# Self attention values: two heads of a pair in one set of PSUM rows, and the norm split over ScalarE, VectorE and GpSimd

## The chip, the cores and the metric

The kernel runs on one core of one Trainium2 chip. The metric is device time in microseconds (us), the median of several executions of the whole program; less is better. Engines: PE is TensorE (matrix products and transposes, results in PSUM), PEld its weight loads, DVE is VectorE, ACT is ScalarE, POOL is GpSimd, SP issues DMAs. Each engine runs its own instructions strictly in the order written and waits at semaphores.

## What is computed

A decoder of four layers on x of 16 batches x 256 rows x 128 columns, in float32; each layer is a self attention, a cross attention and an expert layer. Five attentions over x itself (the first layer's and, beside its cross attention, a second one; the second and the third layer's; and one in the third layer's expert part) have 16 heads of 8 columns. Without their projections, masks, gates and rotary turns they are one function; the third layer applies it three times, each time with the last result as queries:

```
scores = jnp.einsum('bthd,bshd->bhts', q, k * scale) + mask
attn = jax.nn.softmax(scores, axis=-1)
return jnp.einsum('bhts,bshd->bthd', attn, v)
...
context = _self_attention(q, k, v, mask)
for _ in range(REPETITIONS - 1):
    context = _self_attention(context, k, v, mask)
```

## The kernel before, in words

`program` builds stages s0 to s12 and lets each engine run its part of one after the other. Five of the stages are a `SelfAttention`: s0 (rope, no mask), s1 (causal, and 64 rows of cross attention beside it), s3 (a position bias and a gate), s6 (mask added, three repetitions) and s8 (causal, rope). A stage works in units: one batch, all 16 heads; s6 has 48 units (16 batches x 3 repetitions, in groups of four batches, so a unit's next repetition is four units later), the others 16. Two batches are a chunk of 512 rows, for which projections are made. A new unit starts every 8 slots (10 in s1). `pe_slot`, `act_slot`, `dve_slot`, `pool_slot` and `sp_slot` write out what an engine does in slot g: each line there asks whether some unit is now at a given offset. So the offsets fix the order of each queue.

Offsets of a unit: slots 0 to 7, row maxima of the scores, two heads in each slot (`pe_max`, `dve_max`; the score banks handed back by the maxima); slot 9 (`MBT`), the negated maxima are turned (PE L694), copied to `MT` by ACT (L703), and SP copies them beside the queries in `SKB` (`sp_self_shift`, L1245). Slots 12 to 19 (`LE` = 12): scores again with the maxima in them (PE L1452), exponentials (ACT L1412); `pe_pv` (L1505) at 15, 17, 19 and 21 multiplies with the values `VA`, which hold 8 columns and a column of ones a head, so the ninth column is the sum of the softmax.

The results of pv gather in PSUM bank 6 (`PS[:, 6]`), four heads each in rows 32 i to 32 i + 8 of two half banks. When half of the unit's heads are there, ACT copies the bank to `TV` (L718), PE turns it into bank 7 with four transposes (`pe_tvt`, L727), and VectorE makes the reciprocals of the sums (L738) and two products (L744) from bank 7 into `OO`. This happens twice a unit, turns at slot 18 and slot 22. Bank 7 serves all such turns and projections, one after the other: who takes it (`pj_take`) waits for the reader before. In slot `OOS` = 23 (24 with the gate, 26 with cross) PE turns `OO` (L767), ACT copies it to `OT` (L777). Slot OOS + 1 (`OUT`) starts the tail of a chunk: output projection, residual, norm.

Queries and keys are split into three bf16 parts by ACT (`act_hi`, `act_mid`: L638, L644) and GpSimd (`pool_rest`, `pool_lo`: L649, L655), in `HH`, and SP copies them into `SKB` by `stack` (L668), twelve copies a split. In s6 the output `OT` of a unit that has another repetition is split this way in slot OOS and the next; SP's four first copies are step 0 in slot OOS + 1 = 24 (slot 0 of the unit three later), the other eight step 1 in slot 25 (its slot 1). In `sp_slot` the line of the maxima (`MBT`) stands ahead of the steps of a split. The scores of the next repetition wait for the copies to land (`stacked`).

Of the kernel before, what the change touches and what calls it, by code (L numbers as in the profile page):

```python
# [73 lines left out]
class Chip:  # L74


    def __init__(self, nc, A, ctx):
# [19 lines left out]
        self.VA = [sb(f"VA{i}", [128, 64, 9]) for i in range(3)]  # L97
# [3 lines left out]
        self.M3 = [sb(f"M3{i}", [128, 16, 4]) for i in range(2)]  # L101
        self.MB = [sb(f"MB{i}", [128, 2, 32], BF16) for i in range(2)]
# [5 lines left out]
        self.OC = sb("OC", [128, 2, 128])  # L108
# [87 lines left out]
class Begin:  # L196
# [312 lines left out]
class Heads:  # L509
# [222 lines left out]
    def dve_normalise(self, e, f, oo, half):  # L732

        K = self.K
        v = K.PS[:, 7, :].rearrange("p (q x k) -> p q x k", q=2, x=8)
        r = K.RC[f % 2][:, 0:16].rearrange("p (q x o) -> p q x o", q=2, o=1)
        e.wait_ge(*self.tvt.at(f))
        e.reciprocal(r, v[:, :, :, 8:9]).then_inc(*K.dv.inc())  # L738
        e.wait_ge(*K.dv.now())
        v = K.PS[:, 7, :].rearrange("p (q b h k) -> p q b h k", q=2, b=4, h=2)  # L740
        r = K.RC[f % 2][:, 0:16].rearrange("p (q b h o) -> p q b h o", q=2, b=4, o=1)
        out = oo.rearrange("p q (h d b) -> p q h b d", h=2, d=8)
        for par in range(2):
            k = e.tensor_tensor(out[:, :, par, 4 * half:4 * half + 4, :], v[:, :, :, par, 0:8],  # L744
                                r[:, :, :, par, :].to_broadcast([128, 2, 4, 8]), ALU.mult)
# [223 lines left out]
class SelfAttention(Heads):  # L969


    LE, MBT, CMBT, TV, GATE = 12, 9, 11, (5, 9, 11), 8

    def __init__(self, K, prev, W, mode, rope=False, reps=1, gate=False, cross=False, kind="ln", g=None, lead=0, ring=0, begin=None):
# [15 lines left out]
        self.OOS = LE + (14 if cross else 12 if gate else 11)  # L990
        self.OUT, self.TURN = self.OOS + 1, 6 if cross or gate else 5
# [3752 lines left out]
```

## Time and profile before

| | |
|---|---|
| median of 3 runs | 4122.05 us (4118.73 to 4124.15) |
| span of the profiled execution | 4173.4 us, 51 us over the median; no other time of that execution is on record |
| mean granted TensorE clock | 0.870 |
| PE busy | 3222.1 us (77%) |
| DVE busy | 2754.1 us (66%) |
| ACT busy | 2067.0 us (50%) |
| POOL busy | 1179.7 us (28%) |
| units of self attention | 112 (16 + 16 + 16 + 48 + 16) |

The shares are means over stages with different limits; the stretches of the five self attentions stand in the section of rows, each measured from the first scores of its first unit to those of its last. Together they are 1835 us of the span. Numbers behind an arrow in a row name what ended an idle time.

### The profile page before, as it was taken

The page shows a single profiled execution, that of the slowest core. Times are in us where ns is not written, and L with a number is a line of the kernel's source. Part 1 is how long each engine was busy: PE and PEld are TensorE (multiplying, and loading weights), DVE is VectorE, ACT ScalarE, POOL GpSimd, SP SyncE. Part 2 cuts the span into 40 slices and gives each one's busy share as a digit, 9 for nine tenths or more (in the row PEclk, how much of TensorE's full clock was granted, in tenths as well). Part 3 has the DMA queues.
Part 4 walks back from the last instruction along what each step waited for, and adds up shares of the span by engine and source line. Part 5 has one row for each costly group of instructions (what it writes and reads, how often), then busy time and mean ns, then how long its engine had stood idle before and what let it go on. Part 6 is the DMA issues. An engine that isn't in the chain of part 4 may idle for free. (4 is left out here: it accounts for less than half of the span.)

```text
span 4173.4 us, 91912 instructions
## 1 busy us (share of the span) xinstructions
PE 3222.1 (77%) x33262; PEld 2228.3 (53%) x33262; DVE 2754.1 (66%) x7643; ACT 2067.0 (50%) x4648; POOL 1179.7 (28%) x2276
## 2 busy tenths in 40 slices
PE   6886888796888667858898888668865588679881
PEld 2443555473565347745555555335544456579881
DVE  5884667364787575548787787577853769854453
ACT  2664666323444544436787777445630344246551
POOL 2322222012211233451111111243312420334555
PEclk9987899797999778978999999778975799889996
DMA  4323331033221422231212211423420500222332
GB/s 91 70 36 59 54 57 38 16 98 47 35 39 18 64 65 67 76 66 32 49 27 43 41 33 34 64 37 64 62 73 16 168 20 1 82 66 89 88 84 62
DMA packets 321466, 232.56 MB, mean 56 GB/s; under 512 B 46253, under 2 KB 305946, under 8 KB 320838
## 3 DMA queue, kind: packets, MB, share of 16 engines
q1 hardware_dynamic: 307226, 199.40, 23.6%
q0 software_dynamic: 12928, 26.50, 2.2%
q8 instruction: 269, 4.41, 0.5%
q14 instruction: 179, 1.47, 0.1%
q10 hardware_dynamic: 864, 0.79, 0.1%
HBM read 69.21 MB, written 55.63 MB: 30 GB/s over the span
## 5 line engine op out<-in xcount | busy, mean ns | idle before, releaser
L1412 ACT ACTIVATE PT<-ps 128x512 f32<-128x512 f32 (+1 forms) x1600 | 812.1, 560 | 337.1 <-PE ps L1348 241.2
L1362 DVE TENSOR_REDUCE M<-ps 128x2 f32<-128x512 f32 x1024 | 652.5, 683 | 126.2 <-PE ps L1348 102.0
L1314 PE MATMUL ps<-SKB 51*128 51x256 bf16 (+3 forms) x3584 | 414.8, 276 | 117.0 <-DVE M L1362 68.9
L1359 DVE TENSOR_REDUCE M<-ps 128x3 f32<-128x384 f32 x768 | 390.6, 550 | 149.1 <-PE ps L1348 93.0
L1505 PE MATMUL ps<-PT,VA 128*9 128x256 f32 (+1 forms) x7168 | 451.2, 371 | 1.4 <-ACT PT L1412 1.2
L3855 ACT ACTIVATE SKB<-ps,SKB 128x128 f32<-128x128 f32 x1032 | 295.5, 372 | 280.2 <-PE ps L3773 219.5
L1348 PE MATMUL ps<-tri,idh 64*128 64x128 bf16 x5120 | 392.0, 222 | 0.0
L1452 PE MATMUL ps<-SKB 53*128 53x256 bf16 (+3 forms) x3584 | 355.4, 266 | 44.6 <-DMA SKB<-MT 34.7
L3919 DVE COPY SKB<-SKB 128x1028 f32 (+1 forms) x258 | 186.4, 722 | 289.2 <-PE ps L3782 173.4
L1314 PEld LDWEIGHTS ps<-SKB 51*128 51x128 bf16 (+1 forms) x3584 | 131.6, 96 | 386.7 <-DVE M L1362 158.4
L3782 PE MATMUL ps<-SKB 128*128 128x128 f32 x2064 | 288.9, 285 | 30.5 <-ACT SKB L3855 21.8
L1348 PEld LDWEIGHTS ps<-tri,idh 64*128 64x128 bf16 x5120 | 277.8, 98 | 27.5
L3773 PE MATMUL ps<-SKB 128*128 128x128 f32 x2064 | 291.2, 287 | 0.0
L3782 PEld LDWEIGHTS ps<-SKB 128*128 128x128 f32 x2064 | 263.8, 200 | 37.0 <-ACT SKB L3855 25.5
L649 POOL TENSOR_TENSOR FF<-FF,HH 128x512 f32<-128x512 f32 (+1 forms) x118 | 128.7, 1091 | 547.2 <-ACT HH L638 547.1
L3688 POOL DMA_INDIRECT L_sorted_rows<-XT,GG x192 | 197.0, 1026 | 276.6 <-DVE SKB L3926 123.3
L3773 PEld LDWEIGHTS ps<-SKB 128*128 128x128 f32 x2064 | 266.3, 202 | 0.6 <-issue 0.3
L496 POOL TENSOR_TENSOR NW<-NW 128x4 f32<-128x4 f32 x336 | 70.6, 210 | 682.3 <-DVE NW L489 628.1
L1505 PEld LDWEIGHTS ps<-PT,VA 128*9 128x9 f32 x7168 | 155.7, 91 | 165.6 <-issue 35.6
L3748 POOL DMA_INDIRECT PT<-L_sorted_results,GG x192 | 194.1, 1011 | 157.8 <-DVE X L3887 83.9
L727 PE MATMUL ps<-idf,TV 128*128 128x128 f32 x1088 | 180.0, 289 | 52.4 <-ACT TV L718 18.0
L1452 PEld LDWEIGHTS ps<-SKB 53*128 53x128 bf16 (+1 forms) x3584 | 159.2, 96 | 80.7 <-DMA SKB<-MT 38.6
(495 smaller groups left out, 6201.4 us busy)
## 6 DMA issues: line engine op xcount, KB each, us to landing
SKB<-HH SPq DMA_DIRECT2D x1212, 64.0 KB
SKB<-HH SPq DMA_DIRECT2D x576, 32.0 KB
PT<-L_sorted_rows SPq DMA_DIRECT2D x258, 64.0 KB
L_sorted_results<-SKB SPq DMA_DIRECT2D x258, 64.0 KB
SKB<-in_L3f_w SPq DMA_DIRECT2D x32, 256.0 KB
L_sorted_rows<-TV SPq DMA_DIRECT2D x2, 4032.0 KB, 28.9
SKB<-scratch SPq DMA_DIRECT2D x2, 2048.0 KB, 11.5
SKB<-in_L1f_w SPq DMA_DIRECT2D x16, 256.0 KB
```

The lines of the kernel that those rows point to most:

```text
L1314: k = e.matmul(self.mx_bank(m + i)[:, o:o + n], K.QS[self.set(c)][64 * i:64 * i + rows, s, 256 * bb + 128 * qt:256 * bb + 128 * qt + 128], ...
L1348: return e.matmul(blocks[:, :, 64 * sub:64 * sub + 64], K.idh[sub][part, :], tri, start=False, stop=sub == 1)
L1359: k = e.tensor_reduce(K.M3[n % 2][:, hh, 0:3], mx[:, 0:384].rearrange("p (a k) -> p a k", a=3), axis=AX.X, op=ALU.max)
L1362: k = e.tensor_reduce(K.M3[n % 2][:, hh, 0:2], mx.rearrange("p (a k) -> p a k", a=2), axis=AX.X, op=ALU.max)
L1412: e.activation(K.PT[:, x % 4, n * i:n * i + n], self.st_bank(x, i)[:, 0:n], ACT.Exp, bias=0.0, scale=self.scale).then_inc(*self.exp.inc())
L1452: k = e.matmul(self.st_bank(x, i)[:, 256 * kt:512 - lo if kt else 256], k1, q1, start=kt == 0, stop=plain and kt == 1)
L1505: k = e.matmul(K.PS[32 * i:32 * i + 9, 6, 256 * g + lo:256 * g + 256], K.VA[self.set(c)][:, (2 * bb + kt) * 16 + 8 * (i % 2) + 2 * j + i / ...
L3688: e.indirect_dma_start(self.XS[h], bass.IndirectOffsetOnAxis(ap=D.IDX[:, col:col + 1], axis=0), K.XT[:, 128 * t:128 * t + 128], None).then ...
L3748: e.indirect_dma_start(self.YG[i % 8], None, self.YS[h], bass.IndirectOffsetOnAxis(ap=D.IDX[:, q:q + 1], axis=0)).then_inc(*self.gathered. ...
L3773: k = e.matmul(K.PS[:, 2 + m % 2, 128 * hc:128 * hc + 128], self.WT[m % 3][:, 128 * hc:128 * hc + 128], self.XC[m % 3], start=True, stop=True)
L3782: k = e.matmul(K.PS[:, 4 + m % 2, 0:128], self.HB[m % 3][:, hc, :], self.WT[m % 3][:, 512 + 128 * hc:640 + 128 * hc], start=hc == 0, stop= ...
L3855: k = e.activation(self.HB[n % 3][:, hc, :], K.PS[:, 2 + n % 2, 128 * hc:128 * hc + 128], self.func, bias=self.WT[n % 3][:, 1024 + hc:1025 ...
```

## The change

The two halves of a unit's heads now add into the same rows of bank 6: `VA` holds pairs of heads with nine columns of zeros between them, so that a matrix load of 18 columns starting at 0 or at 9 puts the first head's results in the first or the second nine rows and adds zeros to the others. All four pv steps of a unit add up in one bank, with one copy to `TV` and one turn (four transposes) at slot 22. ACT copies the 288 columns that count from bank 7 to `VN` in SBUF (`act_vn`); VectorE takes one reciprocal of 32 columns a row (`dve_recip`), in slot 23 behind that slot's maxima; GpSimd makes four products of 128x64 (`pool_normalise`) in slot 23. The output turn (`OOS`) is in slot 24, 26 with the gate and 27 with cross. With cross, the cross values take the same way with two products on GpSimd.

Other offsets follow: the tail starts at 26 (plain, rope), 31 (gate) or 28 (cross), its turn 5, 8 or 13 slots later; the value projection is made 5 to 8 slots into the chunk's first unit, where it was 13 or 19 slots ahead of it, with two `VA` buffers for three; stages s3 and s8 have four and five slots more. The negated maxima of a unit take two VectorE operations for four. The diff, cut:

```
-        self.VA = [sb(f"VA{i}", [128, 64, 9]) for i in range(3)]
+        self.VA = [sb(f"VA{i}", [128, 32, 27]) for i in range(2)]
...
-        self.OC = sb("OC", [128, 2, 128])
+        self.OV = sb("OC", [128, 288])
+        self.OC = self.OV[:, 0:256].rearrange("p (a b) -> p a b", a=2)
...
+        if order == "self":
+            v = m[:, 0:2, :].rearrange("p q h -> p (q h)").rearrange("p (x b) -> p x b", b=8)
+            o = mb[:, :, :].rearrange("p q r -> p (q r)").rearrange("p (x s b) -> p x s b", s=2, b=8)
+            e.wait_ge(*K.dv.now())
+            e.tensor_scalar(o[:, :, 0, :], v, -1.0, None, ALU.mult).then_inc(*K.dv.inc())
+            e.wait_ge(*K.dv.now())
+            e.scalar_tensor_tensor(out=o[:, :, 1, :], in0=v, scalar=-1.0, in1=o[:, :, 0, :], op0=ALU.mult, op1=ALU.subtract
+                                   ).then_inc(*self.negmax.inc())
+            return
...
-    def dve_normalise(self, e, f, oo, half):
-
-        K = self.K
-        v = K.PS[:, 7, :].rearrange("p (q x k) -> p q x k", q=2, x=8)
-        r = K.RC[f % 2][:, 0:16].rearrange("p (q x o) -> p q x o", q=2, o=1)
+    def act_vn(self, e, f):
+
+        K = self.K
         e.wait_ge(*self.tvt.at(f))
-        e.reciprocal(r, v[:, :, :, 8:9]).then_inc(*K.dv.inc())
-        e.wait_ge(*K.dv.now())
-        v = K.PS[:, 7, :].rearrange("p (q b h k) -> p q b h k", q=2, b=4, h=2)
-        r = K.RC[f % 2][:, 0:16].rearrange("p (q b h o) -> p q b h o", q=2, b=4, o=1)
+        if f > 0:
+            e.wait_ge(*self.nrm.at(f - 1))
+        e.activation(self.VN, K.PS[:, 7, :].rearrange("p (x k) -> p x k", k=32)[:, :, 0:18], ACT.Copy, bias=0.0, scale=1.0
+                     ).then_inc(*self.vn.inc())
+
+    def dve_recip(self, e, f):
+        K = self.K
+        e.wait_ge(*self.vn.at(f))
+        sums = self.VN.rearrange("p x (e k) -> p x e k", e=2)[:, :, :, 8]
+        e.reciprocal(K.RC[f % 2][:, 0:32].rearrange("p (x e) -> p x e", e=2), sums).then_inc(*self.rc.inc())
+
+    def pool_normalise(self, e, f, oo):
+
+        K = self.K
+        v = self.VN.rearrange("p (q b h) (e k) -> p q b h e k", q=2, h=2, e=2)
+        r = K.RC[f % 2][:, 0:32].rearrange("p (q b h e) -> p q b h e", q=2, h=2, e=2)
         out = oo.rearrange("p q (h d b) -> p q h b d", h=2, d=8)
-        for par in range(2):
-            k = e.tensor_tensor(out[:, :, par, 4 * half:4 * half + 4, :], v[:, :, :, par, 0:8],
-                                r[:, :, :, par, :].to_broadcast([128, 2, 4, 8]), ALU.mult)
+        e.wait_ge(*self.rc.at(f))
+        for h in range(2):
+            for half in range(2):
+                k = e.tensor_tensor(out[:, :, h, 4 * half:4 * half + 4, :], v[:, :, :, h, half, 0:8],
+                                    r[:, :, :, h, half:half + 1].to_broadcast([128, 2, 4, 8]), ALU.mult)
+        return k
+
+    def pool_normalise_cross(self, e, f, oo):
+
+        K = self.K
+        v = self.VN.rearrange("p (q b) (h k) -> p q b h k", q=2, h=2)
+        r = K.RC[f % 2][:, 0:32].rearrange("p (q b h) -> p q b h", q=2, h=2)
+        out = oo.rearrange("p q (h d b) -> p q h b d", h=2, d=8)
+        e.wait_ge(*self.rc.at(f))
+        for h in range(2):
+            k = e.tensor_tensor(out[:, :, h, :, :], v[:, :, :, h, 0:8],
+                                r[:, :, :, h:h + 1].to_broadcast([128, 2, 8, 8]), ALU.mult)
         return k
...
-    LE, MBT, CMBT, TV, GATE = 12, 9, 11, (5, 9, 11), 8
+    LE, MBT, CMBT, GATE = 12, 9, 11, 8
+    TV = (9, 11)
...
-        self.OOS = LE + (14 if cross else 12 if gate else 11)
-        self.OUT, self.TURN = self.OOS + 1, 6 if cross or gate else 5
-
-        self.Q, self.KP, self.V = (-30, -20, -13) if cross else (-29, -20, -19) if rope else (-29, -27, -19) if gate else (-25, -15, -19)
-        self.QSTK, self.KSTK = (-26, -17) if cross else (-20, -12) if reps > 1 else (-14, -20) if gate else (-20, -14)
+        self.OOS = LE + (15 if cross else 14 if gate else 12)
+        self.OUT, self.TURN = (28, 5) if cross else (31, 8) if gate else (26, 5) if rope else (26, 8)
+
+        self.Q, self.KP, self.V = (-30, -20, 6) if cross else (-29, -20, 5) if rope else (-29, -27, 8) if gate else (-25, -13, 5)
+        self.QSTK, self.KSTK = (-26, -17) if cross else (-20, -11) if reps > 1 else (-14, -20) if gate else (-20, -14)
...
-        self.nf, self.nm = 2 + cross, 1 + cross
+        self.nf, self.nm = 1 + cross, 1 + cross
...
+        self.VN = (K.GG[:, 0:288] if cross or gate or reps > 1 else K.OV[:, :]).rearrange("p (x k) -> p x k", k=18)
+        self.vn, self.rc = K.ev("values_out", nu * self.nf), K.ev("value_recips", nu * self.nf)
...
-        self.tail.turn_off = 9 if kind == "keep" else self.TURN
+        self.tail.turn_off = 13 if kind == "keep" else self.TURN
...
-        f = self.nf * u + j // 2
+        f = self.nf * u
         x = self.nx * u + 2 * j
-        if j % 2 == 0 and f > 0:
+        if j == 0 and f > 0:
             e.wait_ge(*self.tv.at(f - 1))
         if j == 0 and bb == 0 and self.units[u][1] == 0:
             e.wait_ge(*(self.vact if self.W["vb"] is None else self.vdve).at(c))
         e.wait_ge(*self.exp_done(x + 1))
-        g = j % 2
+        g, half = j % 2, j // 2
         for kt in range(2):
             for i in range(4):
                 lo = 128 if kt == 1 and self.causal else 0
                 o = 256 if kt == 1 else 0
                 pt = K.PT[:, (x + i // 2) % 4, 0:2 * self.width].rearrange("p (a k) -> p a k", a=2)
-                k = e.matmul(K.PS[32 * i:32 * i + 9, 6, 256 * g + lo:256 * g + 256],
-                             K.VA[self.set(c)][:, (2 * bb + kt) * 16 + 8 * (i % 2) + 2 * j + i // 2, :], pt[:, i % 2, o:o + 256 - lo],
-                             start=kt == 0, stop=kt == 1)
+                pair = (2 * bb + kt) * 8 + 4 * (i % 2) + 2 * g + i // 2
+                k = e.matmul(K.PS[32 * i:32 * i + 18, 6, 256 * g + lo:256 * g + 256],
+                             K.VA[c % 2][:, pair, 9 * half:9 * half + 18], pt[:, i % 2, o:o + 256 - lo],
+                             start=j == 0 and kt == 0, stop=j == 3 and kt == 1)
         k.then_inc(*self.pv.inc())
...
+    def pool_norm(self, e, u, h):
         K = self.K
         f = self.nf * u + h
-        if h == 0 and u >= 2:
-            e.wait_ge(*self.oot.at(u - 2))
-        if h < 2:
-            k = self.dve_normalise(e, f, K.OO[u % 2], h)
+        if h == 0:
+            if u >= 2:
+                e.wait_ge(*self.oot.at(u - 2))
+            k = self.pool_normalise(e, f, K.OO[u % 2])
         else:
-            if u > 0:
-                e.wait_ge(*self.oo.at(u - 1))
-            k = self.dve_normalise_cross(e, f, K.OC)
+            k = self.pool_normalise_cross(e, f, K.OC)
         k.then_inc(*self.nrm.inc())
...
-        for h, off in ((0, LE + 6), (1, LE + 10), (2, LE + 12)):
-            u = self.at(g, off)
+        for h, off in enumerate(self.TV):
+            u = self.at(g, LE + off + 1)
             if u is not None and h < self.nf:
-                self.pe_tvt(e, self.nf * u + h, self.nrm.at(self.nf * u + h))
+                self.pe_tvt(e, self.nf * u + h, self.vn.at(self.nf * u + h))
         u = self.at(g, LE + self.GATE)
         if u is not None and self.gate:
...
+                self.act_tv(e, self.nf * u + h, self.pv.at(self.np * u + 2 * h + 3))
         u = self.at(g, self.MBT)
         if u is not None:
             self.act_mt(e, self.nm * u)
+        for h, off in enumerate(self.TV):
+            u = self.at(g, LE + off + 1)
+            if u is not None and h < self.nf:
+                self.act_vn(e, self.nf * u + h)
         u = self.at(g, self.CMBT)
...
-                self.dve_norm(e, u, h)
+                self.dve_recip(e, self.nf * u + h)
...
         if self.begin and g == 60:
             self.begin.all_in(e)
+        for h, off in enumerate(self.TV):
+            u = self.at(g, LE + off + 2)
+            if u is not None and h < self.nf:
+                self.pool_norm(e, u, h)
         u = self.at(g, self.OOS - 1)
```

SP in s6, in its steady order, before: from the last copies of one repetition split to the end of the next (HH: the split parts, MT: the maxima).

```order
L668 DMA SKB<-HH1 8x8x256
L668 DMA SKB<-HH2 8x8x256 [waits split_hi,scores]
L668 DMA SKB<-HH2 8x8x256 x3
L1245 DMA SKB<-MT0 2x8x256 [waits mt]
L1245 DMA SKB<-MT0 2x8x256
L668 DMA SKB<-HH2 8x8x256 [waits split_hi]
L668 DMA SKB<-HH2 8x8x256
L668 DMA SKB<-HH2 8x8x256 [waits split_mid]
L668 DMA SKB<-HH2 8x8x256 x3
L668 DMA SKB<-HH2 8x8x256 [waits split_lo]
```

And after, the same place:

```order
L671 DMA SKB<-HH1 8x8x256
L1281 DMA SKB<-MT0 2x8x256 [waits mt]
L1281 DMA SKB<-MT0 2x8x256
L671 DMA SKB<-HH2 8x8x256 [waits split_hi,scores]
L671 DMA SKB<-HH2 8x8x256 x3
L671 DMA SKB<-HH2 8x8x256 [waits split_hi]
L671 DMA SKB<-HH2 8x8x256
L671 DMA SKB<-HH2 8x8x256 [waits split_mid]
L671 DMA SKB<-HH2 8x8x256 x3
L671 DMA SKB<-HH2 8x8x256 [waits split_lo]
```

The first four copies of a split have moved from ahead of the maxima's two copies to behind them.

PE in s6 around the start of a unit, before (PT, VA: pv; OO: the output turn; SKB in L1314: the scores for the maxima).

```order
L1505 MATMUL ps<-PT,VA 9x256 x7
L767 MATMUL ps<-idf,OO 128x128 [waits normalised]
L767 MATMUL ps<-idf,OO 128x128
L1314 MATMUL ps<-SKB 128x256 [waits mx_free,stacked1]
L1314 MATMUL ps<-SKB 128x256 [waits mx_free]
L1314 MATMUL ps<-SKB 128x256 x2
```

And after, from the start of a unit:

```order
L1354 MATMUL ps<-SKB 128x256 [waits mx_free,stacked1]
L1354 MATMUL ps<-SKB 128x256 [waits mx_free]
L1354 MATMUL ps<-SKB 128x256 x2
L1388 MATMUL ps<-tri,idh 128x2x64 x4
L1492 MATMUL ps<-SKB 128x256 [waits exp]
L1492 MATMUL ps<-SKB 128x256 x3
L1388 MATMUL ps<-tri,idh 128x2x64 x4
L800 MATMUL ps<-idf,OO 128x128 [waits normalised,values_out]
L800 MATMUL ps<-idf,OO 128x128
```

The output turn has moved from ahead of the next unit's first scores to behind that slot's scores.

GpSimd in s8, before (GG: rope add; FF, HH: a split's subtractions; X, RR: residual and its square).

```order
L1170 TENSOR_TENSOR FF1<-FF1,GG 128x512 [waits proj_took]
L649 TENSOR_TENSOR FF1<-FF1,HH1 128x512 [waits split_hi]
L655 TENSOR_TENSOR HH1<-FF1,HH1 128x512 [waits split_mid]
L418 TENSOR_TENSOR X<-X,RR0 128x512 [waits residual]
L419 TENSOR_TENSOR RR1<-RR0 128x512
L1170 TENSOR_TENSOR FF0<-FF0,GG 128x512 [waits proj_took]
```

And after, the place of the same residual (OC holds `VN` in this stage, RC the reciprocals):

```order
L765 TENSOR_TENSOR OO1<-OC,RC1 128x2x4x8 [waits value_recips]
L765 TENSOR_TENSOR OO1<-OC,RC1 128x2x4x8 x3
L1206 TENSOR_TENSOR FF0<-FF0,GG 128x512 [waits proj_took]
L652 TENSOR_TENSOR FF0<-FF0,HH2 128x512 [waits split_hi]
L421 TENSOR_TENSOR X<-X,RR0 128x512 [waits residual]
L422 TENSOR_TENSOR RR1<-RR0 128x512
L658 TENSOR_TENSOR HH2<-FF0,HH2 128x512 [waits split_mid]
L765 TENSOR_TENSOR OO0<-OC,RC0 128x2x4x8 [waits value_recips,oo_turned]
```

The residual and its square have moved between the two subtractions of a split, and the four products of each unit stand behind the split's last one.

## Rows read from the trace of the kernel before

**Rows 1.** Stretches: start:end, us, busy of PE, PEld, DVE, ACT, POOL, clock, DMA.

```profile
71.70:331.70 260.00, 219.87 (x2300) 106.44 (x2296) 219.94 (x569) 175.89 (x336) 71.07 (x128) 0.92 0.34 54
400.60:737.90 337.30, 294.26 (x3988) 183.92 (x3990) 232.26 (x708) 212.10 (x482) 79.63 (x156) 0.93 0.28 49
1017.40:1346.60 329.20, 283.08 (x3210) 195.75 (x3210) 258.76 (x674) 143.21 (x230) 57.99 (x126) 0.96 0.22 31
1906.00:2593.90 687.90, 613.29 (x9687) 381.70 (x9683) 569.02 (x1349) 531.89 (x1049) 98.06 (x182) 0.98 0.19 36
2840.30:3061.20 220.90, 197.44 (x3174) 124.55 (x3172) 178.58 (x480) 145.67 (x332) 69.48 (x119) 0.99 0.34 53
1919.70:1998.30 78.60, 73.17 (x1232) 46.04 (x1228) 69.27 (x156) 66.07 (x132) 8.13 (x12) 1.00 0.12 31
```

**Rows 2.** Timeline of SP in s6: start us, us busy, line, operation, tiles, count.

```profile
1926.94 2.65 SPq L668 DMA_DIRECT2D SKB<-HH  x4
...
1953.11 2.58 SPq L668 DMA_DIRECT2D SKB<-HH  x4
1956.21 1.34 SPq L1245 DMA_DIRECT2D SKB<-MT  x2
1957.60 5.95 SPq L668 DMA_DIRECT2D SKB<-HH  x8
...
2555.67 2.58 SPq L668 DMA_DIRECT2D SKB<-HH  x4
```

**Rows 3.** Line L668, eight issues from 1957.6: who waited (us, times).

```profile
  PEld ps L1314: 0.3, 1
```

**Rows 4.** Waits in all of s6: engine, line, releaser: us in total, times, longest.

```profile
PEld ps L1314 <- DMA SKB<-HH: 2.9, 7, 1.2
```

**Rows 5.** Timeline of PE around two unit starts of s6.

```profile
1952.10 0.39 PE L1314 MATMUL ps<-SKB 51*128 51x256 bf16 x4
...
1962.49 0.63 PE L727 MATMUL ps<-idf,TV 128*128 128x128 f32 x4
...
1964.81 0.44 PE L767 MATMUL ps<-idf,OO 128*128 128x128 f32 x2
1965.30 0.39 PE L1314 MATMUL ps<-SKB 51*128 51x256 bf16 x4
...
1965.97 0.27 PE L1314 MATMUL ps<-SKB 51*128 51x256 bf16 x1
```

**Rows 6.** Timeline of ACT in the same unit.

```profile
1955.83 0.36 ACT L703 ACTIVATE MT<-ps 32x256 bf16<-32x256 bf16 x1
...
1962.49 1.08 ACT L1412 ACTIVATE PT<-ps 128x512 f32<-128x512 f32 x2
```

**Rows 7.** Timeline of DVE in the same unit.

```profile
1963.92 1.28 DVE L1362 TENSOR_REDUCE M<-ps 128x2 f32<-128x512 f32 x2
```

**Rows 8.** Lines by form, steady s6: count, busy us, mean ns, idle before.

```profile
L727 PE MATMUL ps<-idf,TV 128*128 128x128 f32 x48 | 7.7, 283 | 0.9
L718 ACT ACTIVATE TV<-ps 128x512 f32<-128x512 f32 x12 | 7.2, 597 | 0.0
...
L744 DVE TENSOR_TENSOR OO<-ps,RC 128x64 f32<-128x64 f32 x24 | 4.9, 270 | 0.4
...
L738 DVE RECIPROCAL RC<-ps 128x16 f32<-128x16 f32 x12 | 3.0, 247 | 0.0
```

**Rows 9.** Lines by form, whole span, POOL's operations on two tensors.

```profile
L649 POOL TENSOR_TENSOR FF<-FF,HH 128x512 f32<-128x512 f32 x102 | 118.0, 1157 | 475.2 <-ACT HH L638 475.1
...
L496 POOL TENSOR_TENSOR NW<-NW 128x4 f32<-128x4 f32 x336 | 70.6, 210 | 682.3 <-DVE NW L489 628.1 <-issue 35.9
...
L649 POOL TENSOR_TENSOR OT<-OT,HH 128x256 f32<-128x256 f32 x32 | 21.5, 671 | 370.8 <-ACT HH L638 370.8
```

**Rows 10.** Waits in s3.

```profile
PE ps L348 <- ACT MT L703: 13.8, 7, 2.1
```

**Rows 11.** Waits in s1.

```profile
PEld ps L694 <- DVE OO L744: 8.5, 14, 0.9
```

More of the change, by code:

```diff
@@ L101, in __init__ @@
         self.M3 = [sb(f"M3{i}", [128, 16, 4]) for i in range(2)]
+        self.MX3 = [t[:, :, :].rearrange("p a b -> p (a b)").rearrange("p (q h) -> p q h", q=4) for t in self.M3]
         self.MB = [sb(f"MB{i}", [128, 2, 32], BF16) for i in range(2)]
@@ L1267, in values_free @@
     def values_free(self, e, c):
-        if self.leading:
-            self.prev.freed(e, self.set(c))
-        if c >= 3:
-            e.wait_ge(*self.pv.at(self.np * self.last[c - 3] + 3))
+        if c >= 2:
+            e.wait_ge(*self.pv.at(self.np * self.last[c - 2] + 3))
     def act_values(self, e, c):
@@ L1276, in act_values @@
         self.values_free(e, c)
-        e.activation(K.VA[self.set(c)][:, :, 0:8], K.PS[:, 7, :].rearrange("p (a k) -> p a k", k=8), ACT.Copy, bias=0.0,
-                     scale=1.0).then_inc(*self.vact.inc())
+        v = K.PS[:, 7, :].rearrange("p (x e b k) -> p x e b k", e=2, b=4, k=8)
+        va = K.VA[c % 2][:, :, :].rearrange("p (x b) k -> p x b k", b=4)
+        for half in range(2):
+            k = e.activation(va[:, :, :, 18 * half:18 * half + 8], v[:, :, half, :, :], ACT.Copy, bias=0.0, scale=1.0)
+        k.then_inc(*self.vact.inc())
     def dve_values(self, e, c):
@@ L1283, in dve_values @@
         self.values_free(e, c)
-        for i in range(4):
-            k = e.tensor_tensor(K.VA[self.set(c)][:, 16 * i:16 * i + 16, 0:8],
-                                K.PS[:, 7, 128 * i:128 * i + 128].rearrange("p (a k) -> p a k", k=8),
-                                self.W["vb"].rearrange("p (a k) -> p a k", k=8), ALU.add)
+        v = K.PS[:, 7, :].rearrange("p (i h e b k) -> p i h e b k", i=4, h=2, e=2, k=8)
+        vb = self.W["vb"].rearrange("p (o h e b k) -> p o h e b k", o=1, h=2, e=2, k=8)
+        va = K.VA[c % 2][:, :, :].rearrange("p (i h b) k -> p i h b k", i=4, h=2)
+        for h in range(2):
+            for half in range(2):
+                k = e.tensor_tensor(va[:, :, h, :, 18 * half:18 * half + 8], v[:, :, h, half, :, :],
+                                    vb[:, :, h, half, :, :].to_broadcast([128, 4, 4, 8]), ALU.add)
         k.then_inc(*self.vdve.inc())
@@ L1712, in act_slot @@
                 self.act_exp(e, 10 * u + 8 + s, 512, self.pt_free(10 * u + 8 + s))
[L1713 to L1714 removed]
+        for h, off in enumerate(self.TV):
+            u = self.at(g, LE + off)
             if u is not None and h < self.nf:
[L1716 to L1717 removed]
+                self.act_tv(e, self.nf * u + h, self.pv.at(self.np * u + 2 * h + 3))
         u = self.at(g, self.MBT)
@@ L1772, in dve_slot @@
             self.dve_neg_max(e, 2 * u + 1, "cross")
-        for h, off in ((0, LE + 6), (1, LE + 10), (2, LE + 12)):
-            u = self.at(g, off)
+        for h, off in enumerate(self.TV):
+            u = self.at(g, LE + off + 2)
             if u is not None and h < self.nf:
-                self.dve_norm(e, u, h)
+                self.dve_recip(e, self.nf * u + h)
         u = self.at(g, LE + self.GATE)
@@ L1799, in pool_slot @@
             self.begin.all_in(e)
+        for h, off in enumerate(self.TV):
+            u = self.at(g, LE + off + 2)
+            if u is not None and h < self.nf:
+                self.pool_norm(e, u, h)
         u = self.at(g, self.OOS - 1)
```

31 lines of the change are left out of this document (12 added, 19 removed).

## Prediction

> **What bounds the kernel now.** I read the table of stretches first. The five self attentions are s0, s1, s3, s6 and s8; the rest of the span (experts, cross attentions) is not touched. In all five TensorE is the busiest engine, between 219.87 of 260.00 us (s0, level with VectorE) and 613.29 of 687.90 us (s6); in the steady stretch of s6 it is 73.17 of 78.60 us, with VectorE at 69.27, ScalarE at 66.07 and GpSimd at 8.13 [rows 1]. This looks like a kernel that must gain from every TensorE turn and VectorE operation that goes. A unit of s6 takes 78.60 / 6 = 13.1 us there.
>
> But s6 runs three repetitions, and a unit of the second or third needs the output of the unit four before it as its queries. So I read SP's timeline next. In each unit SP issues four copies of the split queries (2.58 us), then the two of the row maxima (1.34 us), then eight more copies (5.95 us) [rows 2]. The unit that starts at 1952.10 has its maxima (MT) at 1955.83 + 0.36 = 1956.19 [rows 5, 6]; SP, in order, starts their copies at 1956.21, the eight at 1957.60, and is done at 1963.55 [rows 2]. The next unit starts at 1965.30 [rows 5], and its first weight load waited 0.3 us for just these copies [rows 3]: they land about 1.75 us after their issue. So MT, 1.4 us of maxima, 5.95 of copies and 1.75 of landing already set that unit's start, and MT in turn follows from the start of its own unit. It is a loop, as long as TensorE's own work. All over s6, 7 of the 32 repetition starts wait for these copies, 2.9 us in all [rows 4]: the loop has little slack. Four issues take 2.58 us, so an eight without a slow issue takes about 5.2, and a start behind such an eight has 5.95 - 5.2, some 0.7 us, to spare, less what it waited here.
>
> **The change part by part.**
>
> *Turns.* One turn of the values a unit goes: four transposes of 0.16 us, 7.7 us for 12 turns, 0.64 each; on ScalarE a 0.60 copy goes and a 288-wide one comes (by width between the 0.36 of MT and the 0.60, so 0.41, my estimate); VectorE loses two reciprocals of 0.25 and four products of 0.27, and two of the four small operations that split the row maxima, and gains one 32-wide reciprocal (0.25 to 0.30) [rows 6, 8]. If every stage were bound by TensorE alone, 112 units x 0.64 = 72 us would go. The pv matmuls keep their number; their loads get 18 columns for 9. I cost that at nothing, because loads overlap and are busy 46.04 of 78.60 us [rows 1]; were they the bound, it would show on every load.
>
> *Products on GpSimd.* No row has a 128x64 product there. From below it is the 128x4 operation, 0.21 us, from above the 128x256 one, 0.67 [rows 9]; on the line between them 0.32. Four in a row: 0.84 to 2.68, I take 1.28. The matching VectorE product takes 0.27 [rows 8]. The Trainium skill speaks against this step (GPSIMD Engine Reference, 4.1 Engine selection): elementwise work on two inputs belongs on VectorE, GpSimd being about twice as slow. By that rule the four would take 8 x 0.27 = 2.16, and the 20 units below would lose another 18 us; the rows put 1.28 nearer, since the fixed 0.21 is most of so small an operation.
>
> *The output turn, one slot later.* In a unit that is not held by the loop, the chain after the turn was: transposes, VectorE, output turn at 1964.81. The turn still starts at 1962.49 and ends at 1963.12; ScalarE's copy comes behind the pair of exponentials that ends at 1963.57, so to 1963.98; the reciprocal comes behind the slot's pair of maxima, 1963.92 + 1.28 = 1965.20, so to 1965.47; the products end at 1966.75 [rows 5 to 7]. TensorE now meets the output turn after the scores of the next slot: 1964.81 + 0.67 (one slot's scores, from 1965.30 to the same place in the next slot) and a little, 1965.6. It would stand 1.1 us. Against that it has the 0.64 of the lost turn, not all of which it can use, because the score banks come free by VectorE's maxima. Net +0.6 a unit (-0.64 where products and waits all hide, +1.1 where none of the turn is gained). There are 20 such units in s6: +12 us (-13 to +22).
>
> *The repetition copies.* The output turn in slot 0 instead of 7 moves the query split one slot. SP then has the maxima's copies, which wait for MT, ahead of the four, as the two orders of SP's issues show. Those 2.58 us, which before ran while SP waited for MT, now come after it: landing is 2.6 us later. Taken off: 0.6 of slack. MT may come up to 0.5 us earlier, as the 0.60 copy ahead of it [rows 6, 8] is gone; twelve issues in a row may hold a slow one more often than eight, up to the same 0.6. So +1.5 to +2.7 a start, and I take +2.05. The pattern four, two, eight stands 29 times in s6, the four first at 1926.94 and last at 2555.67 [rows 2]; 28 starts x 2.05 = +57 us (42 to 76). The output turn's stand is free in these units, because TensorE waits for the landing anyway. What is late next would be nothing: the copies are the last to come. s6 together: +69.
>
> *s0 and s8 (rope).* Each unit also splits a q or k on GpSimd, in three passes over 128x512: the rope add and two subtractions, 1.16 each [rows 9]. The products queue behind the last of them, and in s8 the residual add and the square, two more such passes, now stand between the two subtractions in every second unit. TensorE's output turn waits for that. s0: 16 x 0.64 = -10, and one pass in front of the products, less a little, 1.0 x 16 = +16: +6 (-10 to +16). s8: -10, and in each of 8 pairs of units two passes and a little, 2.6 x 8 = +21: +11 (-10 to +20).
>
> *s3 (gate).* Its output turn gets two slots more, and nothing waits for the products. 16 turns are -10; the output projection leaves the slot in which it waited for MT's copy, 13.8 us over seven chunks [rows 10]. The residual pass and the four value additions now fall in neighbouring slots on VectorE, already busy 258.76 of 329.20 [rows 1]; priced by half a pair of maxima, 0.64, and the product's 0.27 [rows 7, 8] they are 1.7 us x 8 chunks = 14, of which I count a third, +5, on the path. So -19 (-30 to -5).
>
> *s1 (cross).* 16 turns, -10; the wait of the maxima's turn for VectorE's products, 8.5 us [rows 11], goes, but the copy for the cross values waits for GpSimd's first products, +2. So -16 (-22 to 0).
>
> *Ends.* At the end of each of the five stages the chain from the last values to the output is longer by the copy, reciprocal and products less VectorE's norm, about 1.3 us; s3 and s8 also get four and five slots more before the next stage is let in fully. +8 (0 to +15).
>
> Sum: 69 + 6 + 11 - 19 - 16 + 8 = +59. The profiled execution's span is 4173.4, 51 us over the median of 4122; the stretches come from it, and I add the sum to the median: 4181 us, +1.4%.
>
> **The rivals.**
>
> *The loop doesn't bind* (MT over 2 us earlier, or copies that land sooner). Then the 28 units behave like the other 20: +0.6 x 28 = 17 in place of 57: 4122 + 19 = 4141. For it: 25 of 32 starts waited for no copy. Against: the unit that did wait for the eight [rows 3], and SP's fixed order. Chance 0.10.
>
> *Relief wins*: faster. The place is TensorE's queue in the 64 units outside s6; the price is 0.64 us a unit, 41 in all, and the waits in s1 and s3, 22. It decides if the four products take under 0.9 us and GpSimd's splits are through before them, and if MT's half microsecond and the slack leave s6 at only 28 x 1.0 = +28: 4122 - 63 + 28 = 4087. If the loop doesn't bind either, 4060. For it: TensorE is the busiest everywhere. Against: the chain of four engines with one slot to run in. Chance 0.13.
>
> *GpSimd binds*: products at 2.16 and splits ahead of them hold s0, s8 and the free units of s6 for a further us each, 52 units: 4181 + 52 = 4233. Chance 0.09.
>
> *Nothing to measure*: loop at its low end (+42) with s1 and s3 at their best (-52) and the rest near nothing: 4122. Chance 0.06.
>
> **How the numbers follow.** A measurement of this kernel can tell some 0.2%, 8 us, from no change. The forecast has 0.62. Slower: 0.62 + 0.10 + 0.09 = 0.81; same 0.06; faster 0.13. The forecast's own range is 4145 to 4215 (the loop's ends, and half the width of the others). With rival one and the nearer half of the two at the ends it is 4118 to 4225.
>
> **What would show it.** In the changed kernel SP in steady s6 shows two copies of maxima and then twelve of queries without a gap, the first scores of a unit wait about 2 us for the query copies (28 starts, some 50 us, where 2.9 stood), and the period is 15.1 us instead of 13.1, with TensorE's share falling from 93% to about 80. The products show near 0.32 each; the output turns wait for GpSimd in s0, s8 and the first four units of each group in s6; s1 and s3 are shorter by 15 to 20 us. I am wrong if the starts in s6 wait for no copy, if MT comes 2 us sooner, if the products take 0.2 or 0.7, or if idle time lowers the granted clock in s6 below the 0.98 it has now [rows 1].

## The result, and the profile after

The changed kernel takes 4185.7 us (median of 4 runs, 4167.74 to 4202.03) against 4123.1 for the kernel before (4 runs): the ratio is 1.0156, 95% interval 1.0133 to 1.0180. It is slower by 1.6%, 4181 was forecast. The profiled execution has a span of 4165.6 us, 20 under its median, while the one of before was 51 over its own; so the two spans can't be set against each other, but stretches can. The part behind s8's last scores, most of which the change doesn't touch, was 1100.8 us in the profile of before and 1061.9 in that of after: most of what makes the span of before the longer one lies there. In the run e1 below, which has the instructions of before in this part, it was 1059.6.

The five stretches of after, first scores of the first unit to first scores of the last (start:end, us, busy of PE, PEld, DVE, ACT, POOL, granted clock, DMA share, GB/s); they answer [rows 1]:

```profile
72.50:333.90 261.40, 214.09 (x2250) 104.00 (x2248) 207.63 (x463) 176.05 (x335) 85.29 (x174) 0.92 0.34 54
401.60:723.70 322.10, 276.24 (x3934) 176.99 (x3934) 206.07 (x563) 215.18 (x494) 104.61 (x236) 0.95 0.29 51
1004.10:1318.90 314.80, 279.71 (x3148) 191.02 (x3150) 248.07 (x563) 140.06 (x227) 69.36 (x169) 0.93 0.24 32
1863.70:2626.20 762.50, 624.60 (x9504) 384.50 (x9506) 538.95 (x1022) 521.39 (x1049) 146.00 (x354) 0.93 0.16 32
2863.00:3095.00 232.00, 196.56 (x3120) 125.27 (x3115) 162.09 (x374) 145.93 (x339) 82.32 (x174) 0.94 0.32 51
```

| | before | after | difference | forecast |
|---|---|---|---|---|
| s0 | 260.0 | 261.4 | +1.4 | +6 |
| s1 | 337.3 | 322.1 | -15.2 | -16 |
| s3 | 329.2 | 314.8 | -14.4 | -19 |
| s6 | 687.9 | 762.5 | +74.6 | +69 |
| s8 | 220.9 | 232.0 | +11.1 | +11 |

Together +57.5, +51 forecast without the ends. How far the same code differs from profile to profile is seen in the runs below: e1 leaves s0, s1, s3 and s8 as they were before and shows 258.7, 335.3, 336.1 and 223.0 there; e2 and e7 leave s1 as the change made it and show

```profile
402.60:727.10 324.50, 280.49 (x3936) 180.42 (x3938) 206.20 (x563) 215.01 (x494) 104.57 (x236) 0.94 0.29 51
406.90:737.60 330.70, 286.24 (x3934) 182.51 (x3934) 206.52 (x563) 214.40 (x494) 104.54 (x236) 0.92 0.29 50
```

where the table has 322.1. Over these profiles the difference is +1 to +9 us in s0, -5 to -15 in s1, -14 to -23 in s3, +75 to +82 in s6 and +8 to +11 in s8. A difference below some 9 us in a single stretch is not told from none.

In the profile of after, TensorE's busy time fell in every stage but s6, where it rose, 613.29 to 624.60, though 183 of its instructions are gone. The granted clock there fell from 0.98 to 0.93.

SP in a steady unit of s6, after (start us, busy us), answers [rows 2]: the copies of the maxima, then twelve copies of queries without a gap, as the order said.

```profile
2088.57 1.26 SPq L1281 DMA_DIRECT2D SKB<-MT  x2
2089.94 7.90 SPq L671 DMA_DIRECT2D SKB<-HH  x12
```

TensorE in the same unit and at the next start (in brackets, idle time before and what ended it), answers [rows 5]:

```profile
2085.88 0.41 PE L800 MATMUL ps<-idf,OO 128*128 128x128 f32 x2 [1.00 <-POOL OO L765]
...
2086.99 1.06 PE L1546 MATMUL ps<-PT,VA 128*18 128x256 f32 x16
...
2099.57 0.39 PE L1354 MATMUL ps<-SKB 51*128 51x256 bf16 x4 [2.06 <-DMA SKB<-HH]
...
2101.97 1.91 PE L1546 MATMUL ps<-PT,VA 128*18 128x256 f32 x16
```

Two things are to be seen. At 2085.88 the output turn waits 1.00 us for GpSimd's products, in a unit that no copy held up; at 2099.57 the next unit waits 2.06 us for the copies. So it is in all of s6: where a start waits for the copies, the output turn one slot later doesn't wait, and most of the units that no copy holds, the first repetitions of three groups among them, pay at the output turn. The sixteen pv matmuls at 2101.97 take 1.91 us where sixteen such took 1.06 fifteen us earlier. The stretches below go with it; the column behind POOL's is the granted clock. It is 1.00 (2.4 GHz) ahead of the wait, 0.69 in the 4.5 us behind it, and in three of these 0.50 (1.2 GHz).

```profile
2085.90:2096.40 10.50, 10.12 (x172) 6.69 (x172) 8.12 (x15) 9.19 (x20) 1.34 (x2) 1.00 0.11 28
2099.50:2104.00 4.50, 4.43 (x52) 2.54 (x52) 2.77 (x6) 2.75 (x6) 0.67 (x1) 0.69 0.02 5
2101.20:2104.20 3.00, 3.00 (x34) 1.43 (x28) 1.68 (x5) 2.08 (x6) 0.67 (x1) 0.50 0.03 8
```

The clock doesn't fall behind every such wait. The next unit, at 2115.88, waited 2.25 us and kept 1.00. Here are the two units, each from its start to the next, and the copy of the maxima (MT) in each:

```profile
2099.57:2115.88 16.31, 13.34 (x200) 8.07 (x201) 10.77 (x19) 10.77 (x22) 2.44 (x6) 0.90 0.11 28
2115.88:2131.00 15.12, 11.78 (x201) 7.51 (x202) 10.77 (x19) 10.56 (x22) 2.45 (x6) 1.00 0.11 29
...
2104.11 0.37 ACT L712 ACTIVATE MT<-ps 32x256 bf16<-32x256 bf16 x1 [0.89 <-PE ps L703]
2119.43 0.36 ACT L712 ACTIVATE MT<-ps 32x256 bf16<-32x256 bf16 x1
```

Of the 28 units of s6 whose start waited for copies and that another unit follows, 16 ran in part at the lower clock in their first 5 us, and 12 did not. The waits ahead were 1.5 to 3.3 us for the one kind and 1.4 to 2.6 for the other; what decides is not shown. Where the clock fell, MT was there 4.7 to 5.2 us behind the start; where it held, 3.9 to 4.2 (4.1 in a steady unit before). MT opens SP's queue for the twelve copies, so a fallen clock makes the loop itself longer: among the units held by copies at their start and at the next, the 15 with a fallen clock took 16.2 us on average, the 10 with a clock of 1.00 took 15.3.

The waits of s6, after (us in total, times, longest), answer [rows 4], where 2.9 us in 7 starts stood:

```profile
PEld ps L1354 <- DMA SKB<-HH: 81.2, 30, 3.8
PE ps L1354 <- DMA SKB<-HH: 65.2, 29, 3.3
...
PE ps L800 <- POOL OO L765: 14.4, 14, 1.3
```

And what the new operations take, by form in s6 (count, busy us, mean ns); they answer [rows 8, 9]:

```profile
L765 POOL TENSOR_TENSOR OO<-GG,RC 128x64 f32<-128x64 f32 x184 | 50.8, 312 | 387.6 <-DVE RC L754 387.6
...
L747 ACT ACTIVATE GG<-ps 128x288 f32<-128x288 f32 x46 | 19.2, 418 | 0.5 <-PE ps L736 0.5
...
L754 DVE RECIPROCAL RC<-GG 128x32 f32<-128x32 f32 x46 | 16.3, 354 | 1.6
```

### The profile page after: what moved, and what is told of

It is laid out like the page before. It is cut to its first block and busy times, and to the rows that moved or that the text cites. A ratio compares the mean times of both kernels' runs of the same rounds, so it can differ in the third digit from the quotient of the medians.

```text
span 4165.6 us, 90458 instructions
## 1 busy us (share of the span) xinstructions
PE 3176.4 (76%) x32814; PEld 2195.6 (53%) x32814; DVE 2653.9 (64%) x6812; ACT 2055.5 (49%) x4672; POOL 1313.4 (32%) x2756
## 5 line engine op out<-in xcount | busy, mean ns | idle before, releaser
L1546 PE MATMUL ps<-PT,VA 128*18 128x256 f32 (+1 forms) x7168 | 471.1, 384 | 1.6 <-ACT PT L1452 1.6
L3819 PE MATMUL ps<-SKB 128*128 128x128 f32 x2064 | 286.3, 284 | 0.0
L3828 PE MATMUL ps<-SKB 128*128 128x128 f32 x2064 | 280.6, 280 | 3.6 <-ACT SKB L3901 3.6
L765 POOL TENSOR_TENSOR OO<-GG,RC 128x64 f32<-128x64 f32 x320 | 89.2, 315 | 581.1 <-DVE RC L754 581.1
L1546 PEld LDWEIGHTS ps<-PT,VA 128*18 128x18 f32 x7168 | 172.6, 101 | 166.8 <-issue 48.0
## 6 DMA issues: line engine op xcount, KB each, us to landing
SKB<-scratch SPq DMA_DIRECT2D x2, 2048.0 KB, 11.1
```

The lines of the kernel that those rows point to most:

```text
L1546: k = e.matmul(K.PS[32 * i:32 * i + 18, 6, 256 * g + lo:256 * g + 256], K.VA[c % 2][:, pair, 9 * half:9 * half + 18], pt[:, i % 2, o:o + 2 ...
L3819: k = e.matmul(K.PS[:, 2 + m % 2, 128 * hc:128 * hc + 128], self.WT[m % 3][:, 128 * hc:128 * hc + 128], self.XC[m % 3], start=True, stop=True)
L3828: k = e.matmul(K.PS[:, 4 + m % 2, 0:128], self.HB[m % 3][:, hc, :], self.WT[m % 3][:, 512 + 128 * hc:640 + 128 * hc], start=hc == 0, stop= ...
```

## The experiments

Two theories were set against each other for s6. By the loop theory SP's order delays the copies that start a repetition unit. By the chain theory the way of the values over ScalarE, VectorE and GpSimd to the output turn is too long.

**e1: the kernel before, with SP's order of after.** Both steps of a repetition split are issued behind the copies of the maxima.

```
-            u = self.at(g, self.OOS + 1 + step)
+            u = self.at(g, self.OOS + 2)
             if step < 2 and u is not None and self.units[u][1] < self.reps - 1:
```

> The kernel before, with one thing moved: in s6 SP issues the first four copies of a repetition's query split behind the two copies of the maxima, as the changed kernel does; no other engine's work differs. Loop theory (the landing of these copies sets the start of a repetition unit): 28 starts are 2.0 to 2.6 us later, the time is 4123 + 55 to 73 = 4178 to 4196, and the first scores of s6 wait 50 to 80 us for the copies where 2.9 stood. Chain theory (the slower s6 comes from the way over ScalarE, VectorE and GpSimd to the output turn): nothing of that is in this kernel, so within 8 us of 4123.

Measured: 4198.97 us, ratio 1.0199 (1.0179 to 1.0218) to 4119.06 for the kernel before, measured beside it. That is +80 us with no arithmetic changed and s6 alone longer by 84. The stretch of s6 in e1:

```profile
1882.30:2654.40 772.10, 647.99 (x9689) 396.18 (x9687) 570.29 (x1349) 535.25 (x1049) 97.79 (x182) 0.93 0.16 32
```

And its waits for the copies:

```profile
PEld ps L1314 <- DMA SKB<-HH: 59.7, 32, 3.4
...
PE ps L1314 <- DMA SKB<-HH: 50.6, 29, 3.2
```

The order of SP's issues alone is worth more than the whole change loses, and 29 to 32 starts wait, 1.7 us each of TensorE's time. It came out above the expected 55 to 73, and the stretch shows by what: with the same instructions (9689 against 9687 in [rows 1]) TensorE is busy 648 us instead of 613, at a clock of 0.93 instead of 0.98. Of the 84 us, 35 are the same matmuls at a lower clock; the other 49 are idle time, about what the waits for the copies come to (51).

**e2: the changed kernel, with the first four copies ahead of the maxima again.**

```
+        u = self.at(g, self.OOS + 1)
+        if u is not None and self.units[u][1] < self.reps - 1:
+            self.sp_split(e, self.split_of["rep", u], "rep", u, 0)
         u = self.at(g, self.MBT)
         if u is not None:
             self.sp_self_shift(e, u)
...
-            if step < 2 and u is not None and self.units[u][1] < self.reps - 1:
+            if step == 1 and u is not None and self.units[u][1] < self.reps - 1:
```

> The changed kernel, with SP's first four copies of a repetition split ahead of the two of the maxima again (same slot). The split's first part is ready about 1 us after a unit starts, the maxima's copy some 2.4 us after; so the four run in that gap but for about 1.2 us. Loop theory: landing 1.3 to 2 us earlier at 28 to 32 starts, s6 shorter by 36 to 60 us, the time 4126 to 4150. Chain theory: s6 and the time unchanged, 4178 to 4194.

Measured: 4155.46 us, ratio 1.0091 (1.0074 to 1.0108) to the kernel before. The time lies between the two expectations, 5 us over the loop theory's and 23 under the chain theory's. s6 takes 728.4 us, 34 less than in the changed kernel, just under the 36 to 60 expected, and the clock is back at 0.97:

```profile
1868.25:2596.60 728.35, 600.16 (x9502) 372.33 (x9502) 541.67 (x1020) 524.97 (x1049) 146.07 (x354) 0.97 0.17 34
```

TensorE in a steady unit of e2:

```profile
1940.57 0.39 PE L1492 MATMUL ps<-SKB 53*128 53x256 bf16 x4 [0.83 <-DMA SKB<-MT]
...
1948.23 0.41 PE L800 MATMUL ps<-idf,OO 128*128 128x128 f32 x2 [1.01 <-POOL OO L765]
```

The waits of s6 in e2:

```profile
PE ps L1492 <- DMA SKB<-MT: 48.9, 39, 6.5
...
PE ps L800 <- POOL OO L765: 37.4, 38, 1.3
```

The loop is open, and what it covered shows: the output turn now waits 1.0 us for the products in 38 units instead of 14, and the maxima, now behind the four copies, come too late by 0.8 in the steady unit. s6 has both holds. The order alone costs it 84 us (e1, without the saved turn), the chain with the late maxima 40 (e2), both together 75. They don't add up: in the changed kernel a unit that waits for copies at its start has no wait at its output turn. So in the changed kernel undoing the order gives back 34 us of 75, and it stays 0.9% slower than before.

**e3: the changed kernel, with GpSimd's products made twice.**

```
+        k.then_inc(*K.po.inc())
+        e.wait_ge(*K.po.now())
+        for h in range(2):
+            for half in range(2):
+                k = e.tensor_tensor(out[:, :, h, 4 * half:4 * half + 4, :], v[:, :, :, h, half, 0:8],
+                                    r[:, :, :, h, half:half + 1].to_broadcast([128, 2, 4, 8]), ALU.mult)
```

> The changed kernel with GpSimd's four products of a unit made twice (same output): the chain to the output turn is 1.2 to 1.4 us longer in every unit of s0, s3, s6, s8 and by as much for the self heads of s1. Loop theory: hidden in the 28 starts of s6 that wait for copies and in s3 and s1 (room of one or two slots); s0, s8 and the other 20 units of s6 pay 0.8 to 1.3 us each, 52 units: +40 to +65, so 4226 to 4251, with s6 longer by no more than 25 us. Chain theory: all units of s6 pay, s6 longer by 48 x 1.2 = 58 us, the time +95 and more, 4280.

Measured: 4288.37 us, ratio 1.0402 (1.0382 to 1.0422) to before, 103 us over the changed kernel. The total speaks for the chain theory, s6 doesn't. The stretches of s0, s1, s3, s6 and s8 in e3:

```profile
72.80:365.00 292.20, 229.12 (x2250) 111.23 (x2244) 208.85 (x464) 176.19 (x335) 100.74 (x230) 0.85 0.30 49
435.30:776.20 340.90, 288.53 (x3935) 182.85 (x3936) 207.36 (x563) 214.67 (x494) 120.06 (x292) 0.92 0.28 49
1062.20:1377.00 314.80, 276.27 (x3147) 189.58 (x3148) 242.71 (x563) 139.86 (x227) 85.13 (x225) 0.94 0.24 32
1930.10:2723.00 792.90, 638.71 (x9502) 392.80 (x9502) 534.14 (x1020) 523.23 (x1049) 196.79 (x538) 0.92 0.15 31
2961.20:3220.00 258.80, 208.57 (x3118) 130.38 (x3120) 161.71 (x372) 145.79 (x339) 97.56 (x230) 0.90 0.28 45
```

s6 is longer by 30 us, 0.6 a unit and not 1.2: a little over the 25 that the loop theory allowed, and about half of the chain theory's 58. Counted from unit start to unit start, 22 of the 30 fall on the 18 units whose next start doesn't wait for copies, as the loop theory has it. s3 doesn't move: its two slots of room hide the pass. But s0 and s8 lose 31 and 27 us, 1.9 and 1.7 a unit for a pass of some 1.2, and s1, where I had expected room, loses 19. Against e7, which has the same s0 and s1 without the second pass, s0 loses 24 and s1 10. So in s0 and s8 the chain over GpSimd is on the path to its full length and more, in s1 at least in part. The more is again partly the clock, 0.85 in s0 where 0.92 stood; why s1 has no room wasn't followed up.

**e4: the norm of s0, s6 and s8 on VectorE, straight from PSUM.** Merged bank and single turn stay; the output turn is back in slot 23, the keys' offsets in s6 and SP's order there are those of before.

```
+        sums = K.PS[:, 7, :].rearrange("p (x k) -> p x k", k=32)[:, :, 8:18:9]
+        e.reciprocal(K.RC[f % 2][:, 0:32].rearrange("p (x e) -> p x e", e=2), sums).then_inc(*K.dv.inc())
...
+        self.own = not (gate or cross)
+        self.OOS = LE + (15 if cross else 14 if gate else 11 if self.own else 12)
...
+            u = self.at(g, LE + off + 2 - self.own)
...
+                    self.dve_normalise(e, u, K.OO[u % 2]).then_inc(*self.nrm.inc())
```

> The changed kernel with the norm of s0, s6 and s8 back on VectorE, straight from PSUM (one reciprocal of 32 columns, four products, in the slot of the turn), and the output turn in slot 23 as before; the merged bank, the single turn, and all of s1 and s3 stay as changed. Loop theory with the turn's gain: SP's order in s6 is that of before, s0, s6 and s8 keep 0.2 to 0.6 us a unit of the lost turn (80 units, -16 to -48), s1 and s3 keep their -30: 4045 to 4077, faster than both. Rival (the merge itself costs: the 18 column loads, or 1.4 us of VectorE in one slot in place of two of 0.7): s6 at its old 688 us or more, the time 4095 to 4130.

Measured: 4087.51 us, ratio 0.9921 (0.9905 to 0.9938): faster than both the kernel before and the changed one, but between the two ranges expected, by less than the one and by more than the other. s0, s6 and s8 of e4:

```profile
72.90:325.00 252.10, 207.11 (x2250) 101.43 (x2248) 215.17 (x519) 170.34 (x321) 70.18 (x118) 0.95 0.36 56
...
1861.00:2544.70 683.70, 597.22 (x9507) 373.99 (x9502) 557.37 (x1207) 512.99 (x1003) 95.51 (x170) 0.97 0.18 36
2787.20:3018.60 231.40, 198.76 (x3122) 127.26 (x3119) 171.20 (x430) 140.78 (x325) 67.34 (x118) 0.94 0.33 51
```

s0 gains 8 us, half a microsecond a unit, most of the turn's 0.64. s6 gains 4 in 48 units, no more than the same code differs by: TensorE's busy time falls by 16 us, but its waits for VectorE's maxima, which hand the score banks back, take most of that. Before, and in e4:

```profile
PE ps L1314 <- DVE M L1362: 41.3, 86, 1.8
...
PE ps L1371 <- DVE M L1419: 54.6, 128, 1.4
```

And s8 is 231, as in the changed kernel, with no product on GpSimd; so with the tail at its new place it isn't the products that keep s8 long. Its waits for the maxima, 8.4 us before, are now:

```profile
PE ps L1371 <- DVE M L1416: 21.5, 22, 3.0
```

**e6: e4 with the tail of s8 at its old place; e7: the changed kernel with the same.** Two readings of s8 were open: the tail (its residual and square on GpSimd now between two subtractions), or 1.4 us of norm on VectorE at one go.

```
-        self.OUT, self.TURN = (28, 5) if cross else (31, 8) if gate else (26, 5) if rope else (26, 8)
+        self.OUT, self.TURN = (28, 5) if cross else (31, 8) if gate else (24, 5) if kind == "keep" else (26, 5) if rope else (26, 8)
...
-        self.tail.turn_off = 13 if kind == "keep" else self.TURN
+        self.tail.turn_off = 9 if kind == "keep" else self.TURN
```

> The kernel of e4 (VectorE's norm in s0, s6, s8, output turn in slot 23) with the tail of s8 back at its old offsets (output projection in slot 24, its turn 9 slots later). In e4 s8 took 231 us like the changed kernel's 232, though no product runs on GpSimd there; 221 before. Tail theory (the tail's new place, with the square between a split's two subtractions, holds VectorE's maxima and with them TensorE): s8 at 221 or less, since a turn is saved, 211 to 221, the time 4067 to 4080. Norm theory (the 1.4 us of VectorE in one slot hold the maxima): s8 stays at 228 to 234, the time 4085 to 4092.

> The changed kernel with the tail of s8 back at its old offsets (output projection in slot 24, behind the output turn in the same slot; its turn 9 slots later); the products stay on GpSimd. The prediction's step for s8 had two parts, the passes in front of the products and the residual and square among them. If the passes of the split alone are enough, s8 stays at 227 to 234 and the time within 8 us of 4186; if the tail's place made it, s8 falls to 218 to 224 and the time to 4172 to 4180. The output turns wait for GpSimd 24.8 us in s8 now; by the first theory over 15 us of it stay, by the second under 8.

Measured: e6 4071.51 us, ratio 0.9865 (0.9844 to 0.9886) to 4123.29 for the kernel before, measured beside it, the best version here; e7 4212.21, ratio 1.0204 (1.0182 to 1.0227). s8 of e6:

```profile
2788.00:3004.20 216.20, 191.72 (x3122) 122.46 (x3120) 174.77 (x432) 140.52 (x325) 69.39 (x119) 0.98 0.36 54
```

And of e7, with what the output turn waits for there (in the changed kernel 24.8 us, 14 times):

```profile
2893.40:3152.50 259.10, 208.24 (x3118) 131.47 (x3116) 164.16 (x376) 146.82 (x339) 84.21 (x175) 0.90 0.29 45
```

```profile
PE ps L800 <- POOL OO L765: 30.6, 14, 4.0
...
DVE RR L365 <- PE ps L351: 25.0, 7, 4.0
```

With VectorE's norm the tail theory holds: s8 falls from 231 to 216, below the 221 of before. Which of the tail's parts does it, the run doesn't tell: projection, residual, square and turn move together. In e7 neither expectation was met. The output turns wait as long as ever for GpSimd, as the first theory had it, but s8 grows by 27 us: the output projection now stands right behind a late output turn, and VectorE's residual waits for it in its turn. So in the changed kernel the late tail is no fault by itself; it makes room for the late products, and costs s8 what a tail in time would have saved. The two have to be taken together: with the late tail s8 is 231 to 232 with the products on GpSimd or without them; with the old tail it is 259 with them and 216 without. Only without both is it shorter than before.

## Why the prediction was right

**The loop** was the largest term, and e1 shows it by itself: nothing but SP's order moved, +80 us. The sign doesn't hang on it alone. The prediction's own sum without a binding loop was still +19, and e2, with the first four copies ahead again, is 36 us slower than before. The term's working holds in the parts that can be read: twelve issues in 7.90 us without a gap, about 2 us of wait (65.2 us in 29 starts, 2.2 on average, 2.05 forecast), 28 starts forecast and 29 or 30 seen, a period of 15.3 us for 15.1 where the clock held. One reading was off: of the 7 waits in [rows 4], two, at 2057.84 and 2416.35, stand at starts of a first repetition, so 5 of the 32 repetition starts waited before.

What the sum lacked is the clock. "If idle time lowers the granted clock in s6" stood among the things that would make it wrong and had no price; it came, 0.98 to 0.93. TensorE was busy 624.6 us, 24 more than in e2, where the same instructions ran at 0.97. In the time it shows as the 16.2 us of 15 units against the 15.3 of the 10 with a steady clock, some 15 us. Counted from unit start to unit start, after less before, the 29 units that end at a waiting start are longer by 68 us where 57 was forecast, the 18 others by 7 where 12 was. So that s6 is only 6 us over its forecast is in part two errors that cancel.

**The products** were put at 0.32 us on the line between two sizes, and took 0.31; the stand of the output turn at 1.1 in a free unit, and it was 1.00 and 1.01. The rule of the Trainium skill (GPSIMD Engine Reference, 4.1 Engine selection) that two-input work takes GpSimd twice as long isn't borne out at this size: 0.31 against 0.27 on VectorE, which read one input from PSUM. As the prediction argued, most of so small an operation doesn't go with its width: 0.21 at 128x4. Four products in a row took 1.10 us, for 1.28. The copy was 0.42 (0.41 forecast), the reciprocal 0.35, above the 0.25 to 0.30.

**The other stages.** s1 and s3 came out at -15.2 and -14.4 for -16 and -19, and their two waits named in [rows 10, 11] are gone from the lists. That s1 fits so well is luck of the profile: other profiles of the same s1 give as little as -5. s3's gain doesn't hang on the products (e3: 314.8 again). s0 was +1.4 for +6, and its two halves are shown: the turn is worth 8 us (e4: 252.1), and the products take 9 back. s8 was +11.1 for +11, by a step that was half right: the wait for GpSimd is there, 24.8 us for the 21 forecast, but e4 and e6 show that taking it away gains nothing as long as the tail stays at its new place. That the number fits is luck. **The ends**, +8, can't be told from noise: outside of the five stretches the profile of after has 2273 us and e1, with the code of before there, 2268; the stretch from s6's last unit to s8's first was 246 us before, 245 in e1 and 237 after.

The time of 4185.7 for 4181 is thus right by its largest terms and closer than the terms themselves. Of the rivals, "the loop doesn't bind" fell with e1. "Relief wins" fell with the measured time, and e4 shows why it was never large in s6: even with no late product and the old order, the single turn is worth hardly 0.1 us a unit there, and some 0.5 in s0. "GpSimd binds" had its price from products at 2.16 and fell with their 1.10; that the chain over GpSimd is on the path in s0 and s8 e3 shows. "Nothing to measure" fell with a slowdown clear of noise and s6 at +75; its terms, +42 and -52, give 4112 with the rest at nothing, not the 4122 written there.

## What to carry over

Where one in-order queue feeds a loop, moving one producer by a slot can put a blocking wait ahead of copies that had run in its shadow: look at the order of the issuing queue before looking at busy shares. Here e1 priced that at 80 us, with nothing else changed; undone in the changed kernel, where a second chain lay under it, it gave back 30 (e2). A merge that saves the busiest engine a turn pays only where no bank or chain takes it back; the same merge with the norm of s0, s6 and s8 left on VectorE, straight from PSUM, and the old tail in s8 was 1.35% faster than the kernel before (e6).

## What the runs showed of the hardware

After the change, waits of 1.4 to 3.3 us at unit starts of s6 were followed by a fall of the granted clock in 16 of 28 units, in the one shown from 1.00 to 0.50 (2.4 to 1.2 GHz), and by none in 12. There sixteen matmuls took 1.91 us for 1.06; over all of s6 (e1) the same instructions took 35 us more of busy time, beside 51 us of waits.

A small VectorE operation can take many times its length beside GpSimd. Of the first of the two that negate the maxima (L683), 13 of 112 took over 0.6 us after the change, the longest 1.04 where the median is 0.17, and 7 of 320 before, the longest 1.15.

```profile
L683 DVE TENSOR_SCALAR MB<-M x112: 119/172/1043, 67.3 to 3089.0; 128x32 bf16<-128x32 f32 x112
L683 DVE TENSOR_SCALAR MB<-M x320: 159/165/1145, 66.1 to 3055.4; 128x16 bf16<-128x16 f32 x160
...
2229.54 1.04 DVE L683 TENSOR_SCALAR MB<-M 128x32 bf16<-128x32 f32 x1
2229.45 1.09 POOL L345 TENSOR_TENSOR X<-X,WB 128x512 f32<-128x512 f32 x1
```

(First two lines, after and before: count, then shortest, median and longest in ns. Last two, after: one such operation and the pass beside it.) Each of these 20 started while a pass on two tensors ran on GpSimd, 128x512 in 19 of them and 128x256 in one, and ended 0.03 to 0.04 us behind the end of that pass: it waited the pass out. Those beside a 128x512 pass that kept their 0.16 to 0.17 us started ahead of it or in its last 0.12 us. Beside the new 128x64 products, 12 times after the change, none took over 0.6 us. The Trainium skill (GPSIMD Engine Reference, 8. Key points) says that the two engines share their ways into SBUF, with contention for VectorE instructions that have two inputs there or run in a two-port mode. The trace agrees that they get in each other's way; L683 has one input, and no row shows its mode.
